# Three transformer blocks and a rotation: q, k and V projected with tokens on partitions, q and k turned by TensorE

## The reference

```python
h = layernorm(x) * (1 + scale) + shift          # scale, shift, gate from the conditioning
q, k, v = split(h @ W_qkv + b_qkv)              # 16 heads of 9 columns each
attn = softmax(einsum("blhd,bmhd->bhlm", q, k) * 9 ** -0.5)
x = x + gate * (einsum("bhlm,bmhd->blhd", attn, v) @ W_proj + b_proj)
h = layernorm(x) * (1 + scale2) + shift2
x = x + gate2 * mlp(h)                          # layer 1: a mixture of 4 experts, top 2
# after layer 2: U = qr(P), R = expm(skew(cond)), x = x + ((x @ U) @ R - x @ U) @ U.T
```

## Time and profile before

| | before |
|---|---|
| median of 3 runs | 1422.37 us |
| the profiled execution | 1420.17 us |
| its span | 1418.3 us |
| PE busy, share of the span | 93% |
| PEld | 77% |
| DVE | 72% |
| ACT | 53% |
| POOL | 59% |
| mean granted clock of TensorE | 0.965 |

### The profile page before, as it was taken

One profiled execution on the slowest core, in us unless ns is written; L12 is line 12 of the kernel. 1 busy time (PEld: TensorE's weight loads), 2 busy tenths in 40 slices (PEclk: granted clock), 3 DMA queues, 4 the chain that ended last, 5 costly groups with the idle time before them and its releaser, 6 DMA issues.

```text
span 1418.3 us, 37913 instructions
## 1 busy us (share of the span) xinstructions
PE 1313.8 (93%) x14090; PEld 1093.3 (77%) x14090; DVE 1016.5 (72%) x2588; ACT 746.5 (53%) x1507; POOL 843.3 (59%) x2444
## 2 busy tenths in 40 slices
PE   3799999969989999998999999999889999988997
PEld 2588888758877778877888888888778888866775
DVE  6699999955569999994556545645489999975422
ACT  2367676646546766765333333332356766665451
POOL 4656566566666665665666656677777777770000
PEclk9699999989989999998999999999989999999997
DMA  6221221232351211113111111242333333331120
GB/s 153 39 16 15 18 18 16 43 89 30 31 126 13 16 14 19 15 16 64 5 13 14 12 6 12 16 30 10 16 25 23 23 24 23 23 27 21 22 59 26
DMA packets 50878, 41.93 MB, mean 30 GB/s; under 512 B 9018, under 2 KB 46317, under 8 KB 50264
## 3 DMA queue, kind: packets, MB, share of 16 engines
q0 software_dynamic: 4224, 7.45, 15.7%
q1 hardware_dynamic: 45695, 29.91, 9.4%
q10 hardware_dynamic: 780, 2.17, 0.5%
HBM read 29.14 MB, written 2.99 MB: 23 GB/s over the span
## 4 chain that ended last, share of the span: by engine, by line
PE 80%; DVE 13%; issue 4%; ACT 2%; SPq 1%; DMA 1%; DVEq 0%; ACTq 0%
PE PS L1266 17%; PE PS L1515 16%; PE PSA L1266 13%; PE PSA L1322 7%; PE PS L1346 6%; PE PS L1358 3%; DVE BIG L515 3%; PE PS L1366 2%; PE PSB L1491 2%; PE PS L1376 2%; PE PS L1377 2%; PE PSB L1266 1%; PE PS L1371 1%; PE PS L1280 1%; DVE KK L503 1%
## 5 line engine op out<-in xcount | busy, mean ns | idle before, releaser
L1127 ACT ACTIVATE BIG<-PSA 128x512 f32<-128x512 f32 (+1 forms) x224 | 131.9, 594 | 297.0 <-PE PSA L1266 296.9
L1515 PE MATMUL PS<-w,BIG 128*128 128x144 f32 (+1 forms) x1920 | 256.3, 288 | 15.4 <-DVE BIG L752 8.0
L1515 PEld LDWEIGHTS PS<-w,BIG 128*128 128x128 f32 (+1 forms) x1920 | 246.2, 191 | 23.6 <-issue 9.6
L1035 ACT ACTIVATE BIG<-PSB 128x1024 f32<-128x1024 f32 x192 | 196.9, 1025 | 111.4 <-PE PSB L1329 110.7
L515 DVE TENSOR_REDUCE BIG<-PSA 128x8 f32<-128x1024 f32 x192 | 234.0, 1219 | 19.9 <-PE PSA L1322 16.2
L1026 ACT ACTIVATE qkhi<-PS 128x512 fp32r<-128x512 f32 x188 | 112.3, 597 | 102.0 <-PE PS L1266 92.5
L1322 PE MATMUL PSA<-KK,Q 32*128 32x128 f32 x1536 | 132.1, 291 | 12.5 <-DVE Q L503 6.3
L1322 PEld LDWEIGHTS PSA<-KK,Q 32*128 32x128 f32 x1536 | 104.7, 192 | 48.3 <-issue 21.7
L1266 PE MATMUL PS<-hhi,Ahi 128*128 128x256 f32 x376 | 128.4, 342 | 14.1 <-DVE h L473 9.8
L1715 POOL MEMSET qprod<- 128x2 f32 x63 | 6.2, 99 | 218.2 <-DMA QB<-QA 218.2
L1329 PE MATMUL PSB<-Q,KK 32*128 32x128 f32 x1536 | 129.4, 286 | 0.0
(11 more groups left out here) (285 smaller groups left out, 3590.2 us busy)
## 6 DMA issues: line engine op xcount, KB each, us to landing
gate<-gates SPq DMA_DIRECT2D x96, 72.0 KB, 2.9
mgate<-gates SPq DMA_DIRECT2D x96, 72.0 KB, 2.8
X<-in_x SPq DMA_DIRECT2D x4, 576.0 KB, 14.9
out<-X SPq DMA_DIRECT2D x8, 288.0 KB, 3.7
BIG<-in_skew_w SPq DMA_DIRECT2D x2, 1024.0 KB
w<-in_w SPq DMA_DIRECT2D x1, 1440.0 KB, 8.4
BIG<-in_wqkv SPq DMA_DIRECT2D x2, 584.0 KB
BIG<-in_wm SPq DMA_DIRECT2D x1, 1154.0 KB
```

The source lines that it names most:

```text
L1035: S.activation(PT[:, u % 2, a, :], PSB[:, :], ACT.Exp, scale=float(HD) ** -0.5).then_inc(exp_done, 1)
L1127: S.activation(hm[0:rows, slot, :], PS[(par * FTOT[l] + j) % 2][0:rows, :], gelu).then_inc(gelu_done, 1)
L1515: last = mm(o, hm[0:rows, slot, s * 128:(s + 1) * 128], w2[0:rows, FT * e + k, :], start=(k == 0), stop=(k == FT - 1))
```

## The change

The weights of q, k and V are kept compact (9 columns a head, 432 in all, `WC`), taken out of the padded rows that are loaded as before. All three are projected with h on the array: for each batch s of a pair one `split_product` of 4 matmuls of 432 columns. ScalarE spreads q and k rounded to 32 columns a head in the SBUF tile `qt` (`qkv_high`) and copies them to the second place that the high part has in a head's 32 columns (`qt_dup`); VectorE writes the low part and copies V (`qk_low`); TensorE turns `qt` in 4 transposes for q (even j) and 4 for k (`qk_turned`), into the bank where the product stood; ScalarE copies each turned bank to Q or KK (`qk_copy`). The output of the product, and the turned q and k, all stand in PS[4], but for the first pair of a layer, where PS[3] serves too.

The diff, cut to its core:

```diff
@@ setup: banks and weights
-        def qk_bank(pn, j):
-            return PS[4 if pn % NP or j % 2 == 0 else 6 if pn == 0 else 3]
+        def qkv_bank(pn, s):
+            return PS[3 if pn % NP == 0 and s else 4]
+        def turn_bank(pn, j):
+            return PS[3 if pn % NP == 0 and j == 1 else 4]
@@ VectorE
+                (qk, v), (qk3, v3) = compact(wr, C0), compact(wr3, S3)
+                V.tensor_tensor(lo, qk, hi.bitcast(F32), ALU.subtract)
+                V.tensor_tensor(Alo[:, 2 * C:WC], v, Ahi[:, 2 * C:WC].bitcast(F32), ALU.subtract).then_inc(a_split, 1)
...
-                def qk_stack(pn, par, j):
-                def values(P, par):
+                def qk_low(pn, s):
+                    dve.wait_ge(qk_hi, 2 * pn + s + 1)
+                    if pn == NP * l:
+                        dve.wait_ge(va_set, (1, 1, 3)[l])
+                    ps = qkv_bank(pn, s)[:, 0:2 * C].rearrange("p (k h w) -> p k h w", k=2, h=NH)
+                    for k, at in ((0, 2 * HD), (1, HD)):
+                        last = V.tensor_tensor(qt[:, s, k, :, at:at + HD], ps[:, k], qt[:, s, k, :, 0:HD].bitcast(F32), ALU.subtract)
+                    last.then_inc(qk_lo, 1)
+                    V.tensor_copy(VA[:, (2 * pn + s) % 4, :, 0:HD], ...).then_inc(v_ev, 1)
@@ ScalarE
-                def qk_high(n):
+                def qkv_high(pn, s):
+                    act.wait_ge(qkv_ps, n + 1)
+                    wait(act, qk_turn, 4 * pn - 2 + 2 * s if pn else 0)
+                    S.activation(qt[:, s, :, :, 0:HD], src, ACT.Copy).then_inc(qk_hi, 1)
+                    act.wait_ge(qk_hi, n + 1)
+                    S.activation(qt_dup[s], qt[:, s, :, :, 0:HD].bitcast(F32), ACT.Copy).then_inc(qk_dup, 1)
+                def qk_copy(pn, j):
+                    act.wait_ge(qk_turn, n + 1)
+                    wait(act, s2_done, 4 * (pn - 2) + 2 * s + 2)
+                    S.activation((Q, KK)[j % 2][:, pn % 2, :, s * 128:(s + 1) * 128], ...).then_inc(qk_rd, 1)
@@ ScalarE, pair
                     if at(1):
                         exps(e - 2, e % 2, 0)
-                    if at(0):
-                        qk_high(4 * pn + 3)
                     if 0 <= i + 1 < NL:
                         h_high(i + 1)
+                    if at(0):
+                        qk_copy(pn, 3)
...
                     if 0 <= i + 2 < NL:
                         h_modulate(i + 2)
+                    if at(-1):
+                        qk_copy(pn + 1, 2)
@@ TensorE
+                def qkv_product(P, s):
+                    pn = NP * l + P
+                    pe.wait_ge(h_ready, n_h(l, 0) + P + 1)
+                    if P:
+                        pe.wait_ge(qk_rd, 4 * pn + 2 * s)
...
+                    split_product(qkv_bank(pn, s)[:, 0:WC], (Ahi, Alo, AW3), slice(0, WC), P % 2, s * 128, 128,
+                                  weights_moving=True).then_inc(qkv_ps, 1)
+                def qk_turned(P, j):
+                    pe.wait_ge(qk_lo, 2 * pn + s + 1)
+                    pe.wait_ge(v_ev, 2 * pn + s + 1)
+                    pe.wait_ge(qk_dup, 2 * pn + s + 1)
...
+                        pe.wait_ge(qk_rd, 4 * pn + j - (P == 0 and j == 2))
+                    for g in range(G):
+                        last = nc.tensor.transpose(turn_bank(pn, j)[:, g * 128:(g + 1) * 128], qt[:, s, j % 2, 4 * g:4 * g + 4, :]..., ident)
@@ TensorE, pair
                     if at(1):
                         pv(e - 2, (e - 2) % 4, 0)
                     if now:
-                        v_product(i, i % 2)
+                        qk_turned(i, 3)
                     if at(2):
                         project(o - 4, o % 2)
...
@@ TensorE, before the gate products of the setup
-                    pe.wait_ge(qk_lo, 4)
+                    pe.wait_ge(qk_turn, 3)
                     gate_products()
```

More of the change, by code:

```diff
@@ L20 @@
 WQKV = 2 * G * 128 + C
+WC = 3 * C
 FF = 4 * C
@@ L980, in qkv_cast @@
                 act.wait_ge(ld_wq, 112 * (l + 1))
-                wait(act, v_ps, NP * l)
-                S.activation(Ahi[:, :], wr, ACT.Copy).then_inc(a_cast, 1)
-                S.activation(AW3[0:S3, :], wr3, ACT.Copy).then_inc(a_cast, 1)
+                wait(act, qkv_ps, NB * l)
+                for t, (qk, v) in ((Ahi, compact(wr, C0)), (AW3[0:S3, :], compact(wr3, S3))):
+                    S.activation(t[:, 0:2 * C].rearrange("p (h w) -> p h w", w=HD), qk, ACT.Copy)
+                    S.activation(t[:, 2 * C:WC], v, ACT.Copy).then_inc(a_cast, 1)
             def setup_rest():
@@ L1084, in pair, with next_first @@
                             high(1, 1)
+                    if at(-1):
+                        qk_copy(pn + 1, 1)
                     if at(0):
                         exps(e, e % 2, 1)
-                    if at(-1):
-                        qk_high(4 * pn + 6)
+                    if at(-1) and i >= 0:
+                        qkv_high(pn + 1, 1)
                     if 0 <= i + 2 < NL:
                         h_modulate(i + 2)
-                return pair, h_modulate, h_high, qk_high
+                    if at(-1):
+                        qk_copy(pn + 1, 2)
+                return pair, h_modulate, h_high, qkv_high, qk_copy
             def mlp(l, nxt):
                 if nxt:
-                    next_pair, next_modulate, next_high, next_qk_high = nxt
+                    next_pair, next_modulate, next_high, next_qkv_high, next_copy = nxt
+                def next_first():
+                    for s in range(2):
+                        next_qkv_high(NP * (l + 1), s)
+                    for j in range(3):
+                        next_copy(NP * (l + 1), j)
+                    next_modulate(1)
                 gelu = ACT.Gelu if l == 2 else ACT.Gelu_apprx_tanh
@@ L1143, in mlp_step @@
                     if m + 1 == NM:
-                        for j in range(3):
-                            next_qk_high(4 * NP * (l + 1) + j)
-                        next_modulate(1)
+                        next_first()
                 def x_copy(q):
@@ L1282, in turn @@
                     last.then_inc(xt_done, 1)
-                def qk_product(P, par, j):
-                    n = 4 * (NB // 2 * l + P) + j
-                    if j == 0:
-                        pe.wait_ge(h_ready, n_h(l, 0) + P + 1)
-                        if P == 0:
-                            pe.wait_ge(a_split, 2 * l + 2)
-                    if n == 1:
-                        pe.wait_ge(q_at, 1)
-                    if l == 1 and n % (4 * NP) == 1:
-                        pe.wait_ge(sk_ev, 2)
-                    wait(pe, qk_lo, n - 1 if P == 0 and j > 1 else n)
-                    for gg in range(2):
-                        g = 2 * (j % 2) + gg
-                        w0 = (1 - j // 2) * G * 128 + g * 128
-                        last = split_product(qk_bank(n // 4, j)[:, gg * 256:(gg + 1) * 256], (Ahi, Alo, AW3), slice(w0, w0 + 128), par, 0, 256)
-                    last.then_inc(qk_ps, 1)
```

157 lines of the change are left out of this document (85 added, 72 removed).

## The result

The changed kernel takes 1472.89 us (median of 4 runs, 1470.01 to 1483.53) where the kernel before, in the same job, took 1422.48 (1419.52 to 1423.13): a ratio of 1.037 with a 95% interval of 1.032 to 1.043, slower. The profiled execution took 1470.01 us with a span of 1468.2. The forecast was 1480, with 1463 to 1502 as its own range.

What follows compares the result with a forecast made beforehand. In attention TensorE and VectorE were taken as full at once, and added waits outweigh TensorE's 1.36 us less work a pair. 1420.2 + 67 (attention) - 7 (setup) = 1480 us, range 1463 to 1502.

Steps and rivals of the forecast that it cites:

- 1, `pv` late: Start of a pair: exponentials queue behind ScalarE's copy of the third turn, so `pv` starts at 1.22, not 0.84: +0.38 us.
- 2, scores behind `project`: `oT_copy` queues behind ScalarE's copy of the fourth turn; `project` starts at 3.43 instead of 2.37, a further +0.68 us.
- 3: Scores, product, `out_back`, scores after `project`: the first scores' maximum ends in time for the later scores, a gain of 0.15 us.
- 4, even `max_turn`: VectorE's subtraction, three operations and maximum set the even `max_turn`, 2.78 behind the scores where it was 2.76: +0.02 us.
- 5, product of s=1: The second turn and its copy release the product for s=1, 2.99 behind `max_turn` instead of 2.25: +0.74 us.
- 6: From the product of s=1 through the scores to the next odd `max_turn`, which the maximum sets: -0.15 us.
- The attention: All layers' attention: 44 of 48 pairs counted at 15.90 instead of 14.38 us each, +67 us, bounds 53 to 88.
- The clock: Rival: a tenth of the attention pairs run at 1.2 GHz, +40 us and more, 1520 or above; chance 0.05.
- The setup: Before the first pairs: gate products no longer wait behind VectorE, shorter first products and weight split; -7 us, between -2 and -11.
- The layer changes: MLPs between the layers' attentions: the compact weight casts lie beside TensorE's work, counted as 0.
- TensorE-bound: Rival: handoffs hide behind other work, a pair takes 13.0 to 13.8 us, total 1398 to 1400 us; chance 0.10.
- balance: Rival: waits cancel the saving, a pair takes 14.4 us, only the setup's gain remains, 1413 to 1416 us; chance 0.07.

Runs made afterwards that it cites:

- e1: Changed kernel with ScalarE's copy of the fourth turn moved behind `oT_copy`; 1413.46 us, ratio 0.996, a pair 14.56 instead of 15.82.
- e2: Changed kernel with ScalarE's copy of the third turn moved behind the exponentials that open the next pair; 1437.25 us, ratio 1.016.
- e3: Changed kernel with both ScalarE copies moved, the fourth turn's behind `oT_copy` and the third's behind the next pair's exponentials; 1390.97 us, ratio 0.980.
- e4: Changed kernel without writing or waiting for `qt_dup`, so low-times-high products are missing from the scores; 1481.16 us, ratio 1.043.
- e8b: The kernel of e3, unchanged, run again in a later job with more rounds; 1386.04 us, ratio 0.977.
- e7: Changed kernel with the gate products waiting again for VectorE's sixteen statistics; 1478.06 us, ratio 1.041.
- e9: Changed kernel with idle ScalarE copies and VectorE subtractions, 1000 columns each per layer, restoring about the old cast and split length; 1477.98 us, ratio 1.041.
- e5: Changed kernel with eight unread TensorE products of 128 columns as filler in the wait ahead of `project`; 1464.47 us, ratio 1.031.
- e6: Changed kernel with eight unread TensorE transposes as filler in the wait ahead of `project`; 1459.38 us, ratio 1.031.
- e8: e3 with VectorE's maximum ahead of `qk_low` and `added`, and TensorE's `max_turn` and `project` ahead of the next pair's first turn; 1399.1 us, ratio 0.984.

## Why the prediction was right, and where it was off

The mechanism is the one forecast: two copies on ScalarE, each ahead of something that TensorE waits for. e1, e2 and e3 show it by taking them away, and e4 excludes the amount of ScalarE's work. The terms of a pair, from the rows above (offsets from the odd `max_turn` at 198.20) against the earlier trace rows:

| step | forecast | measured |
|---|---|---|
| 1, `pv` late | +0.38 | +0.46 (1.30 for 0.84) |
| 2, scores behind `project` | +0.68 | +0.76 (4.21 for 2.99, less step 1) |
| 3 | -0.15 | -0.17 (6.22 for 5.17) |
| 4, even `max_turn` | +0.02 | -0.22 (8.76 for 7.93) |
| 5, product of s=1 | +0.74 | +0.83 (11.84 for 10.18) |
| 6 | -0.15 | -0.24 (15.80 for 14.38) |
| sum | +1.52 | +1.42 |

Step 4 was off most. VectorE in the same pair, beside the earlier trace rows:

```profile
205.04 0.51 DVE L522 TENSOR_TENSOR qt<-PS,qt 128x144 fp32r<-128x144 f32 x2
205.47 0.30 DVE L524 COPY VA<-PS 128x144 f32<-128x144 f32 x1
205.69 1.22 DVE L529 TENSOR_REDUCE BIG<-PSA 128x8 f32<-128x1024 f32 x1
```

The subtraction starts 0.62 behind the scores at 204.42, where I had 0.82, and the 0.65 for three operations is as forecast (0.66); so TensorE waits 0.46 there, not 0.6. The removal experiments give more than steps 1 and 2 of the table, 1.68 against 1.22, and both are right: with the waits gone TensorE shows a turn of 0.50 where the V product took 0.96 (e8b has its scores 2.53 behind `max_turn`, before it was 2.99), a saving that the waits had hidden. In one place the prediction contradicts itself: it first says that the V product fills no wait, and in step 2 that it was the cover of `project`. The second is right in part: `oT_copy` ended at 183.94, 0.31 after the V product began.

By the large terms:

- *The attention*, +67 forecast. Found +73: 13 us at 1.2 GHz, 4 more in layer 1's pair after its third `turn` (19.76 us for 15.71, much of it at 1.2 GHz; 15.0 and 15.9 with the fillers), less 3 in the first pairs counted here (20.82 to 18.90, 23.65 to 22.72), and 59 for the rest. That is below 67 because a pair lost 1.42, not 1.52, and pairs that stood at 14.5 to 14.8 before lost less still.
- *The clock*, to which I gave a chance of 0.05 at 1520 or more. It came in part. My argument was that a pair that is 82% busy stays at 2.4 GHz, since the 1.83 of 2.50 us of the earlier trace rows do. I took the mean pair. In layer 1's pairs with casts `pv` waits 1.49 and `project` 0.99 within 3.8 us, because casts hold ScalarE's queue for 1.15 us (475.27 to 476.42) ahead of exponentials that are already late; in those of layers 0 and 2 `pv` waits 0.77. Two falls came in each kind, and none in a pair without a cast behind the first pairs of a layer. The step that failed is the one from the mean pair to the worst. That the waits bring the falls is supported, not proved: the profiles of the kernels with all waits (changed, e4, e7, e9) have 4, 6, 3 and 6 such pairs, those with one wait moved or filled (e1, e2, e5, e6) 1, 1, 1 and 0, and those with both moved (e3, e8b, e8) none; but each is one execution, and the executions differ. Why the fall comes at the wait that ends at 494.42 and not at its twin 17 us earlier isn't settled.
- *The setup*, -7 forecast, -11 found, at the end of my bounds; e7 puts 7.6 of it at the gate products, which start at 34.15 instead of 41.54:

```profile
34.15 0.57 PE L1270 MATMUL PS<-mgate,sc 128*32 128x216 f32 x8
```

- *The layer changes*, 0 forecast, -12.4 found: the largest error of mine. I said that the compact casts lie beside TensorE's work and did not price the first pairs at all. e9 gives the casts 2.0. The first pairs of layers 1 and 2 give 8.6 (16.64 to 15.12, 18.26 to 14.80, 26.04 to 22.38). In the second of these stretches, the trace of before has 2.0 us of waits of the scores for the last subtraction, and forty products (32 of 256 columns, 8 of 144) where eight of 432 and sixteen transposes stand now; that is read from the traces and was not tested. The 1.8 us left lie in the second MLP and are open.

So +67 - 7 was in fact +59 + 17 - 3 - 11 - 12 = +50. Against the profiled execution the forecast was 10 us high: the pairs cost 8 less than forecast, the setup gained 4 more, the first pairs counted gained 3 and the layer changes 12, and against these 27 stands the unforeseen loss of 17. That the total lies inside the range is in part luck, and says less for the reasoning than the pair of 15.80 does.

The rivals: *TensorE-bound* and *balance* were false for this order of the queues; another order comes near the first. TensorE in e8b over the window of the earlier trace rows, columns as there:

```profile
150.00:200.00 50.00, 46.70 (x662) 36.10 (x660) 42.61 (x98) 41.16 (x85) 29.57 (x85) 1.00 0.22 18
```

TensorE still waits: 0.30 and 0.46 for the two maxima and 0.18 for `qk_copy` ahead of the second product. Without these 0.94 us the pair of 14.14 would take 13.2, close to the 13.02 of work in the prediction. That kernel takes 1386 to 1391 us, less than the 1398 to 1400 of the rival. The cap of 22 us, up to QR's end, was taken from one execution; QR ended anywhere from 1254.5 to 1272.9 in the twelve profiles, so the cap was anything from 22 to 40 us.

## What to carry to other kernels

When a copy that waits for TensorE is put into an engine's queue, look at what stands behind it: here one such instruction cost 1.26 us a pair and two moved lines made a change from 3.7% slower to 2.3% faster. Before judging a rewrite of the data path by its time, walk one period of it and try the copies behind whatever the bounding engine needs next. And take the clock from the pair with the longest waits, not from the mean.

## What the hardware showed that I had not expected

- TensorE's clock went from 2.4 to 1.2 GHz for 6.8 to 13.7 us, though no single wait in these pairs was above 1.5 us; in the 5 us just before the four falls it had been busy 3.0, 3.2, 2.4 and 2.9 us. The Trainium skill (TensorE: Matmul & The Clock Gate, Part 1, "A second HAM failure mode") describes, for a bf16 kernel that cycles through PSUM banks, falls of the clock by frequent short idle times; these traces agree with that in kind.
- QR on GpSimd, with the same number of GpSimd instructions in every kernel, ended at 1257.5 us in e8b and at 1266.6 in e3, one kernel: 9.1 us apart. So the 9 us between before (1272.9) and after (1263.8) need not be an effect of the change. They are not shown to be none either: the other ten profiles lie between 1254.5 and 1266.6, and only the kernel before ends later.
